# Attention and pooled-attention block on one core: four edits at the first and last images (wake-up products, score groups, pairs of weighted sums, output banks)

## The reference

```python
# layer 0: ordinary attention, 8 heads of 16, all 1024 tokens against all 1024
x_norm = (x - mu) * rsqrt(var + EPS) * ln_scale + ln_bias
q, k, v = split(x_norm @ w_qkv + b_qkv)
attn = softmax(einsum('bqhd,bkhd->bhqk', q, k) * HEAD_DIM ** -0.5)
x = x + einsum('bhqk,bkhd->bqhd', attn, v) @ w_out + b_out
# layer 1: tokens attend to the 16 best of 64 pooled positions, then a feed-forward part
tokens = x @ Win + b_in
t = layernorm(tokens);  q, k, v = t @ Wq, t @ Wk, t @ Wv
pk, pv = pool2d(k), pool2d(v)                  # means over 4 x 4 fields: 64 positions
red = einsum('bhsd,bhpd->bhsp', q, pk).max(axis=(1, 2))
_, top_idx = top_k(red, 16)                    # the same 16 positions for all heads
tokens = tokens + softmax(q @ sel_k * scaling) @ sel_v
tokens = tokens + gelu(layernorm(tokens) @ Wf1 + bf1) @ Wf2 + bf2
return tokens @ Wout + bout
```

## Time and profile before

| | |
|---|---|
| median of 3 runs | 807.12 us (805.31 to 808.18) |
| the profiled execution's own time | 804.28 us |
| its span | 802.6 us |
| busy, share of the span | PE 757.7 (94%), ACT 604.1 (75%), DVE 503.7 (63%), POOL 160.5 (20%) |
| exponentials, line 904 | 512 instructions, 491.7 us |
| weighted sums, line 651 | 2048 records, 255.9 us |
| scores, line 636 | 1024 records, 217.0 us |
| mean granted TensorE clock | 0.991 |

### The profile page before, as it was taken

The page is one execution under the profiler, slowest core; times in us unless marked ns, Lnnn a source line. Parts: engine busy times, 40 slices in busy tenths (PEclk is TensorE's granted clock), DMA queues, the critical chain, the costliest instruction groups (busy, mean ns, idle before and its releaser), DMA issues.

```text
span 802.6 us, 14186 instructions
## 1 busy us (share of the span) xinstructions
PE 757.7 (94%) x5001; PEld 362.6 (45%) x5001; DVE 503.7 (63%) x1512; ACT 604.1 (75%) x686; POOL 160.5 (20%) x198
## 2 busy tenths in 40 slices
PE   8889989999999999999999999999999998998967
PEld 6322333345443545345443545344453544333655
DVE  6413545677667775678657775677736784466764
ACT  4597769787897788887897788878887867877313
POOL 2620503410340111410331212410310201100000
PEclk9899999999999999999999999999999999999989
DMA  3554243532433342522514333422414422400100
GB/s 72 99 85 81 51 67 70 107 52 43 93 73 73 54 67 54 123 51 42 105 44 91 66 58 64 112 49 47 79 38 102 67 48 47 107 13 2 32 1 27
DMA packets 44733, 51.32 MB, mean 64 GB/s; under 512 B 15729, under 2 KB 33777, under 8 KB 44657
## 3 DMA queue, kind: packets, MB, share of 16 engines
q1 hardware_dynamic: 44656, 50.35, 32.5%
HBM read 5.45 MB, written 4.19 MB: 12 GB/s over the span
## 4 chain that ended last, share of the span: by engine, by line
PE 60%; ACT 17%; issue 5%; DVE 5%; ACTq 0%; DVEq 0%
PE O L651 20%; PE S L636 15%; ACT Pr L904 12%; PE BC L665 6%; PE BC L780 3%; PE BC L657 3%; PE BC L706 2%; PE BC L684 2%; PE BC L765 2%; PE A L589 2%; PE A L665 1%; ACT hT L953 1%; ACT tT L919 1%; ACT L904 1%; ACT L953 1%
## 5 line engine op out<-in xcount | busy, mean ns | idle before, releaser
L904 ACT ACTIVATE Pr<-S 128x1024 f32<-128x1024 f32 x512 | 491.7, 1029 | 115.7 <-PE S L636 112.0
L651 PE MATMUL O<-Pr,Va 128*32 128x512 f32 x2048 | 255.9, 604 | 1.4 <-DVE OT L1130 0.7
L636 PE MATMUL S<-Qs,Ks 49*128 49x512 f32 x1024 | 217.0, 470 | 22.7 <-ACT Pr L904 20.4
L636 PEld LDWEIGHTS S<-Qs,Ks 49*128 49x128 f32 x1024 | 87.7, 185 | 178.7 <-ACT Pr L904 145.7
L651 PEld LDWEIGHTS O<-Pr,Va 128*32 128x32 f32 x2048 | 49.8, 109 | 104.9 <-issue 97.2
L1130 DVE STREAM_TRANSPOSE OT<-O 128x512 f32<-128x512 f32 x32 | 22.8, 713 | 54.2 <-PE O L651 54.0
L1235 DVE TENSOR_REDUCE r<-BC 128x1 f32<-128x512 f32 x56 | 36.0, 683 | 17.7 <-PE BC L706 17.7
L509 POOL TENSOR_TENSOR squares<-qh 128x1024 bf16<-128x1024 f32 x7 | 13.3, 1893 | 158.4 <-DVE hot L1257 117.4
L478 POOL TENSOR_SCALAR xn<-X,ln 128x128 f32<-128x128 f32 x56 | 44.0, 799 | 3.6 <-DVE ln L1043 3.6
L517 POOL TENSOR_TENSOR q1l<-q1T,q1h 128x1024 fp32r<-128x1024 f32 x7 | 16.7, 2384 | 135.3 <-DVE q1h L1187 135.3
L531 POOL TENSOR_TENSOR tokx<-tokx_new,tok_bias 128x1024 f32<-128x1024 f32 x8 | 18.9, 2366 | 120.1 <-DVE tokx_new L1049 120.1
(11 more groups left out here) (232 smaller groups left out, 980.3 us busy)
## 6 DMA issues: line engine op xcount, KB each, us to landing
Qs<-qh SPq DMA_DIRECT2D x128, 64.0 KB, 2.3
Ks<-kh SPq DMA_DIRECT2D x128, 64.0 KB, 2.3
Q1s<-q1h SPq DMA_DIRECT2D x56, 128.0 KB, 2.4
X<-in_x_dram SPq DMA_DIRECT2D x8, 512.0 KB, 4.4
Qs<-ql SPq DMA_DIRECT2D x64, 64.0 KB, 2.4
Ks<-kl SPq DMA_DIRECT2D x64, 64.0 KB, 2.3
attnT<-On SPq DMA_DIRECT2D x128, 32.0 KB, 2.0
out_dram<-Y SPq DMA_DIRECT2D x16, 256.0 KB, 2.7
```

The costliest lines, as they stand in the source:

```text
L636: mm = pe.matmul(S[:, c, a * HALF:(a + 1) * HALF], Ks[head, j, kb * P:(kb + 1) * P], Qs[head, j, c * HALF:(c + 1) * HALF], start=True, sto ...
L651: mm = pe.matmul(O[r:r + 32, :], Va[:, kb, 2 * j + a, :], Pr[:, (STEPS * n + s) % 3, c, a * HALF:(a + 1) * HALF], start=(kb == 0), stop=(k ...
L904: act.activation(Pr[:, g % 3, c, :], S[:, c, :], ACT.Exp, scale=SCALE).then_inc(probs_ready, 1)
```

## The change

There are four edits, and one of them carries others with it.

1. **Wake-up products.** `WAKE` goes from 24 products of 128 columns to 9 of 512 columns.
2. **Image 0.** The tasks of a step stand between its two score groups instead of behind the sums, at all steps whose number isn't a multiple of 8 (`tasks_between`).
3. **Image 7.** `sums_behind` names pairs of sums up to step 14 (`FULL`), and single sums behind it.
4. **Image 6's output.** `wout` and `out` use the banks `A` and `O` instead of `BC0` and `BC1`. PE waits ahead of it for the last drains of `A` and `O`, and `last_scores` waits until DVE has drained them to `Y`. DVE alone does the steps 4 to 8 of image 7 (with `norm1`, which makes `that`, line 1146) ahead of the rest of image 6. `WARM` changes: 4 pairs instead of 8 at `t`, 5 instead of 8 at the scores, 8 new ones at `rt`, 6 instead of 4 at `sel`, 10 instead of 12 at `pt`; ahead of those at `rt` PE waits for DVE's maximum over `S` (`last_read`).

```diff
-def tail():
+def tail(held=0):
...
-    return before[:k] + last[:m] + before[k:] + last[m:]
+    return before[:k] + last[:m + held] + before[k:] + last[m + held:]
...
-    if n in (0, IMAGES - 1) or (n == 1 and s < LIGHT):
+    if n == 0 or (n == 1 and s < LIGHT) or (n == LAST and s > FULL):
         return (s - 1,) if s > 0 else ()
...
+def tasks_between(n, s):
+
+    return n == 0 and s % TILES > 0
...
-WARM = {ENDING.tok: 4, ENDING.t: 8, ENDING.pk: 2, ENDING.sc[0]: 8, ENDING.sel: 4, ENDING.pt: 12, ENDING.t2: 10}
-WAKE = 24
+WARM = {ENDING.tok: 4, ENDING.t: 4, ENDING.pk: 2, ENDING.sc[0]: 5, ENDING.rt: 8, ENDING.sel: 6, ENDING.pt: 10, ENDING.t2: 10}
+WAKE = 9
...
                 if s == at.wout and n < LAST:
...
+                    if n == LAST - 1:
+                        pe.wait_ge(a_drained, len(a_turn_of))
+                        pe.wait_ge(o_turned, PAIRS * IMAGES)
+                    for h in range(2):
+                        bank = OUT_BANKS[h] if n == LAST - 1 else b_turn(n, K_OUT + h)[0]
...
-                pe.wait_ge(a_drained, len(a_turn_of))
-                pe.wait_ge(o_turned, PAIRS * IMAGES)
+                pe.wait_ge(last_out, 2)
...
+                pe.wait_ge(last_read, 1)
...
             for _ in range(WAKE):
-                pe.matmul(FIRST[4][:, 0:P], ident[:, :], ident[:, :], start=True, stop=True)
+                pe.matmul(FIRST[4].rearrange("p (a b) -> p a b", a=4), ident[:, :], ident[:, :].unsqueeze(1).to_broadcast([P, 4, P]),
+                          start=True, stop=True)
...
+                for s in range(STEPS):
+                    scores(n, s, 0)
+                    if tasks_between(n, s):
+                        tasks(s)
+                    scores(n, s, 1)
+                    for behind in sums_behind(n, s):
+                        weighted(n, behind)
+                    if not tasks_between(n, s):
+                        tasks(s)
...
-                    dve.wait_ge(last_filled, 1)
-                    dve.tensor_reduce(r8[:, 0:1], S[:, :, :].rearrange("p c q -> p (c q)"), AX.X, ALU.max)
+                    dve.wait_ge(last_filled, 3)
+                    dve.tensor_reduce(r8[:, 0:1], S[:, :, :].rearrange("p c q -> p (c q)"), AX.X, ALU.max).then_inc(last_read, 1)
...
-            for n, s in tail():
+            for n, s in tail(ENDING.norm1 - ENDING.tok):
                 after_tasks(n, s)
```

More of the change, by code:

```diff
@@ L57 @@
 AT_BOUND, AT_FLAG = 28, 30
-LIGHT = 13
+LIGHT, FULL = 13, 14
 After = namedtuple("After", "tok norm1 t q1 pk sc rt rb sel s2 exp2 e2 pt tok2 norm2 tt2 t2 ff gelu wout out")
@@ L122, in b_uses @@
                 (at.tt2, K_TT2, 2), (at.t2, K_T2, 2))
-    return ((at.tok, K_TOK, 2), (at.t, K_T, 2), (at.q1, K_Q1, 2), (at.pk, K_PK, 2),
+    uses = ((at.tok, K_TOK, 2), (at.t, K_T, 2), (at.q1, K_Q1, 2), (at.pk, K_PK, 2),
             *((at.sc[j], K_SC + 2 * j, 2) for j in range(PAIRS)), (at.rt, K_RT, 1), (at.rb, K_RB, 1), (at.sel, K_SELK, 2),
@@ L126, in b_uses @@
             *((at.ff[f], K_FF + 2 * f, 2) for f in range(2)), (at.wout, K_OUT, 2))
+    return uses[:-1] if n == LAST - 1 else uses
 def b_turns():
@@ L261, in two_layers @@
         last_filled, last_ff, last_out = sem("last_filled"), sem("last_ff"), sem("last_out")
+        last_read = sem("last_read")
         sp_passed, pool_passed, pe_passed, dve_passed = sem("sp_passed"), sem("pool_passed"), sem("pe_passed"), sem("dve_passed")
@@ L370, in store @@
                 for h in range(2):
-                    if n == LAST:
-                        sp.wait_ge(last_out, h + 1)
+                    if n >= LAST - 1:
+                        sp.wait_ge(last_out, 2 * (n - LAST + 1) + h + 1)
                     else:
@@ L767, in after_tasks @@
                 if s == at.wout and n < LAST:
+                    if n == LAST - 1:
+                        pe.wait_ge(a_drained, len(a_turn_of))
+                        pe.wait_ge(o_turned, PAIRS * IMAGES)
                     for h in range(2):
-                        bank, filled = b_turn(n, K_OUT + h)
+                        bank = OUT_BANKS[h] if n == LAST - 1 else b_turn(n, K_OUT + h)[0]
                         for t in range(4):
@@ L774, in after_tasks @@
                     h = at.out.index(s)
-                    bank, filled = (OUT_BANKS[h], last_filled) if n == LAST else (BC[h], b_filled[h])
+                    bank, filled = (OUT_BANKS[h], last_filled) if n >= LAST - 1 else (BC[h], b_filled[h])
                     for f in range(2):
@@ L860, in image, with tasks @@
                     pe.sem_inc(max_turned, 1)
[L861 to L865, removed]
+                def tasks(s):
                     if n > 0:
@@ L1224, in after_tasks @@
                     for i in range(2):
-                        dve.wait_ge(last_filled, 2 + i)
+                        dve.wait_ge(last_filled, 4 + i)
                         ins = dve.tensor_reduce(r8[:, 3 + i:4 + i], OUT_BANKS[i][:, :], AX.X, ALU.max)
@@ L1305, in after_tasks @@
                     h = at.out.index(s)
-                    if n == LAST:
-                        dve.wait_ge(last_filled, 4 + h)
+                    if n >= LAST - 1:
+                        dve.wait_ge(last_filled, (1 if n < LAST else 6) + h)
                         bank, drained = OUT_BANKS[h], last_out
```

## The result

The kernel before took 807.04 us (median of 4 runs, 805.31 to 808.18), the changed one 798.91 us (4 runs, 797.54 to 800.51). The ratio is 0.9912, 95% interval 0.9889 to 0.9936; that is 7.1 us, where the two medians by themselves are 8.1 apart. So the steps are compared one by one, from the start of one instruction to that of another.

What follows compares the result with a forecast made beforehand. PE, busy 94% of the span, was taken to lead, with waits at the ends. Terms -0.7 + 3.1 + 3.6 + 1.1 + 1.6 = 8.7 us less, from the median 807.12 to 798.4; range 794.5 to 802.6.

Steps and rivals of the forecast that it cites:

- Image 0: Tasks between score groups fill PE's wait for ACT; two steps with a task take 4.56 us, not 5.02; 3.1 gained.
- The rival in which ACT's gaps count in full: Image 0 is bound by ACT, not PE: gain 1.0 instead of 3.1 us, time 800.5; chance 13%.
- The second half of v (step 29): In image 0, one of five tasks of the same kind, each to gain 0.46 us.
- Image 7: Pairs of sums cover PE's waits of about 0.4 us for ACT after each task, as in image 6; 3.6 us gained.
- The wait for q1 that I had priced at 0.3: Image 7, step 17: q1 transfers must land first and nothing shortens them; 0.3 us taken off the 3.9.
- The wake-up products: At the start: the 9 longer products end at 12.1, 0.7 us behind 11.42; 0.7 us lost, passed on to everything.
- The equation of the prediction: Start: x / 0.213 + (8.41 - x) / 0.107 = 48, for when the clock rises to full; about 5.6 us.
- what the prediction gave only to its low end: Start: the clock may fall in the wait ahead of 11.42, slowing q, k and v; not in the sum.
- if their number counted: Start: the clock rises by number of products, so none of 18 records runs fast; 5.5 us lost, 803.2; chance 4%.
- The tail, first part: `that` comes ahead of the drains of `Y`, and fewer `WARM` pairs let `last_scores` start earlier; 1.1 us gained.
- The tail, second part: Pairs at `rt` and `sel` keep the clock up: 1.0 us from the first half layer-1 scores, 0.6 from small products.
- The rival had the fall right: Tail: the clock falls all the same, pairs at `rt` end 1.5 us late; 4.2 worse, 802.6; chance 12%.

Runs made afterwards that it cites:

- the pairs alone: Only the pairs of sums in image 7 up to step 14 (`FULL`) added to the kernel before: 802.23 us, ratio 0.9950.
- three kernels with the old tail: The kernel before with one edit each: wake-up products (804.55 us), tasks between image 0's score groups (803.24), pairs of sums in image 7 (802.23).
- the last kernel: Changed kernel plus own semaphore for the first three q1 transfers, `last_scores` filling `S` last, 14 pairs at `rt`, 2 at `rb`, 8 at `sel`: 797.78 us, ratio 0.9897.
- the second measurement of both: The unaltered changed kernel timed again against the kernel before, for a second profile: 798.73 us, ratio 0.9921.
- the kernel with the gaps at `rb` and `sel`: Changed kernel with `last_scores` filling `S` last, DVE reading `O` and `A` first, 14 pairs at `rt` into those banks: 798.19 us, ratio 0.9919.
- image 0 with pairs: Changed kernel with image 0 done like the middle images, pairs of sums at even steps and tasks behind them: 819.07 us, ratio 1.0168.

## Why the prediction was right, and where a step of it was not

The time, 798.91, is 0.5 us from the forecast of 798.4 and inside its range. The terms:

**Image 0: forecast 3.1, measured 2.9.** Free of falls of the clock, the image takes 75.6 and 75.8 us in the old order (the wake-up edit alone; the pairs alone) and 72.7 to 72.8 in the new one (seven profiles). The step is as reasoned: 4.55 us for the two steps, forecast 4.56, no wait for ACT, and PE sets the pace. The rival in which ACT's gaps count in full is out. Two terms were off and cancelled, which is luck. The second half of v (step 29) was to give 0.46, and steps 28 and 29 take 5.13 us against 5.05: PE had no wait there that the task could fill. The transposes at step 10 were to give nothing, and steps 10 and 11 take 4.81 against 5.26.

**Image 7: forecast 3.6, measured 2.9 less a wait of 0 to 1.4.** The steps 0 to 16 gave 3.3 of the sum's 3.9. "The rest of the image is unchanged" was wrong: steps 16 to 20 take 0.4 more even where nothing waits for q1. Up to the last exponential the image takes 92.13 us before, and 89.20 and 89.25 in the two profiles that have neither a fall of the clock in it nor a wait above 0.1; the pairs alone gave the same 2.9. The wait for q1 that I had priced at 0.3 ("less than one such wait") is mis-sized: 0 to 1.37 us by execution, 0.8 in the mean of the eight profiles. Its place was named, its spread wasn't, since before showed only one execution.

**The wake-up products: forecast 0.7 lost, measured none to be seen.** The equation of the prediction gives 6.6 us and not 5.6; in the records of before's profile the pace changes at 7.48, 5.9 us behind the start, so the value used was the better one. The loss is real when the clock rises late. In three of eight profiles with the 9 products (18 records in 10.7 to 10.9 us) the transposes started 0.7 to 0.9 us late, the clock fell at 24, and the first scores came at 29.2 to 29.4. In the five others the transposes started at 11.4 to 11.6 all the same, there was no such fall, and the first scores came at 27.5 to 27.9. Against it stands what the prediction gave only to its low end. With the 24 small products PE waited 1.4 to 2.8 us ahead of the first half image, and the clock fell behind that wait, at 11 to 18, in four of five profiles (before's own is the fifth); with the 9 long ones in none of eight. The first scores started at 28.7 in the mean of the five and at 28.3 in that of the eight. So the term should have been about nothing, with that fall in the sum; 0.9999 for the edit alone fits. The Trainium skill ("TensorE: Matmul & The Clock Gate", in "What's actually happening") makes the warm-up a matter of time and says that it varies from run to run. The runs agree: 18 records would have taken until 16.9 if their number counted, and ended between 11.0 and 12.5.

**The tail, first part: forecast 1.1, measured 1.0.** The mechanism held: `that` comes ahead of `Y`, and `last_scores` waits for DVE. From `that` to the maximum over `S` it takes 9.45 us against before's 9.49, so nearly all that was won is that `that` comes earlier: 3.62 us, of which 2.64 came with the end of image 7. That leaves 1.0, and from the last exponential to `that` every profile with the new tail is 1.0 shorter than every one with the old (15.4 against 16.4). One link was missing: `last_scores` is released by DVE's copy of `pkv`, which ends 0.3 us behind `K1s`.

**The tail, second part: forecast 1.6, measured nothing.** This is the step that failed: "The clock should then stay up". From the maximum over `S` to the second drain of `E` it takes 20.52 us in the changed kernel's first profile and 20.63 before; from `last_scores` on, the six profiles with the new tail and the four with the old have 22.1 and 22.0 in the mean. The rival had the fall right, but not its price: the pairs at `rt` ended ahead of the transposition in spite of it, or at most 0.2 late, and those at `sel` cost 0.4 where the clock fell early (4.59 us from the transposition of `r` to `bd_k`, against 4.19 in three kernels with the old tail), not 1.5 and 1.1.

The size was nearly right for a clock that stays up: counted from `last_scores` the stretch is 21.65 us before, 22.1 to 22.2 in three kernels with the old tail, and 20.45 in the last kernel, 1.2 to 1.7 less. Against before, 0.9 of the 1.2 is the first half of the layer-1 scores (forecast 1.0) and 0.4 the small products (forecast 0.6). What it takes to keep the clock up is not settled. Eight pairs, started only when DVE had read `S`, left PE idle for 1.7 us in front of them and for three gaps of 0.5 to 0.6 behind; the profile in which the clock stayed up has the first at 0.75 and the others at 0.3 or less. But six executions of that kernel had a fall somewhere, and two of the kernel with the gaps at `rb` and `sel` had none.

**The sum.** 0 + 2.9 + 2.9 + 1.0 + 0 is 6.8 us, less 0.8, the mean of the eight waits for q1: 6.0, against 8.7 forecast. The two ratios of the changed kernel give 7.1 and 6.4, each uncertain by about 2. So the forecast was some 2 us too good. That the median came within 0.5 us of it is luck in good part: the kernel before took 807.04 us in that measurement and 805.2 to 805.9 in the four later ones, and the second measurement of both has their medians 6.5 apart, not 8.1.

## What to carry to other kernels

Move a task to where the engine waits already, and put two sums together only where tasks fill the step without any: the same pairing gained 3 us in the image full of tasks and lost 18 in the empty one. Work that only keeps the clock up has to be priced over several executions: here it gained 1.2 to 1.7 us in the one profile in which it left hardly a gap up to the work that it was meant for, nothing in the mean of those in which it covered half, and once the clock had fallen it ended late. And when an engine gets faster, look at the transfer that used to come just in time, over several executions.

## What was not expected of the hardware

The place at which the clock falls changes from execution to execution of one kernel: in the tail at 768 in one profile of the changed kernel, near 760 in the other. At the start the same 18 records took between 9.46 and 10.88 us, and the same 48 between 7.05 and 8.41. No single long wait is needed: before the fall in the tail of the changed kernel PE's longest idle time was 1.7 us, and in image 0 with pairs it fell time and again with waits of up to 1.6 us between the products.

Each profile has a few single DMA issues that take up to 2.1 us where the median of 56 is 0.59. Of SP's 719 issues in an execution 16 to 24 take over 1.1 us, and some places recur: in 12 of the 14 profiles the 577th or the 578th is one of them, with 1.2 to 1.7 us. The profiles show no cause for them.
